# Cross attention of a fused decoder layer: y double-buffered, its scaling and its affine part issued one step earlier

## The reference, cut to what matters

```python
delta = ctx @ Wo.T + bo
delta = rs * delta                       # rs: a clipped scalar
mu, var = delta.mean(-1), ((delta - mu) ** 2).mean(-1)
delta = (delta - mu) / sqrt(var + EPS_LN) * ln_gamma + ln_beta
x2 = layernorm(x1 + delta)               # x1: the input of this block
```

## Time and profile before

| what | value |
|---|---|
| median of 3 executions | 1508.37 us (1506.76 to 1509.74) |
| the profiled execution, its own time | 1507.78 us |
| its span, first to last instruction | 1505.6 us |
| mean granted TensorE clock | 0.974 of full |
| busy: PE, DVE, ACT, POOL | 1398.6, 1206.9, 802.0, 675.5 us |

### The profile page before, as it was taken

One profiled execution on the slowest core, in us unless ns is written; L12 is line 12 of the kernel. 1 busy time (PEld: TensorE's weight loads), 2 busy tenths in 40 slices (PEclk: granted clock), 3 DMA queues, 4 the chain that ended last, 5 costly groups with the idle time before them and its releaser, 6 DMA issues.

```text
span 1505.6 us, 25440 instructions
## 1 busy us (share of the span) xinstructions
PE 1398.6 (93%) x8598; PEld 1098.3 (73%) x8610; DVE 1206.9 (80%) x1979; ACT 802.0 (53%) x1798; POOL 675.5 (45%) x760
## 2 busy tenths in 40 slices
PE   8999999999999999999999999879999998359986
PEld 6888888888888888888888888767777776223332
DVE  6888888888888888888878888636788888669996
ACT  6444444544444445455555565445555665258884
POOL 6534334334335244334333433342445443448984
PEclk9999999999999999999999999989999999679998
DMA  7301101201101011011121111230000004014433
GB/s 267 113 15 43 57 15 30 68 1 42 40 31 42 28 43 29 22 50 56 36 82 66 35 42 35 79 112 15 15 15 15 14 1 175 0 35 91 95 79 93
DMA packets 73477, 79.95 MB, mean 53 GB/s; under 512 B 46102, under 2 KB 46614, under 8 KB 72988
## 3 DMA queue, kind: packets, MB, share of 16 engines
q1 hardware_dynamic: 73372, 78.73, 17.3%
HBM read 59.83 MB, written 8.40 MB: 45 GB/s over the span
## 4 chain that ended last, share of the span: by engine, by line
PE 53%; DVE 29%; issue 9%; POOL 5%; ACT 2%; DMA 1%; DVEq 1%; POOLq 0%; SPq 0%; ACTq 0%
PE psum L342 10%; PE psum L344 9%; PE psum L343 9%; DVE rope_b L541 6%; PE psum L990 4%; PE psum L991 4%; PE psum L992 4%; DVE total_e L554 3%; PE psum L386 3%; DVE acc L584 3%; DVE p L550 3%; DVE s L522 2%; PE psum L1058 2%; PE psum L407 2%; DVE rope_a L541 2%
## 5 line engine op out<-in xcount | busy, mean ns | idle before, releaser
L774 POOL TENSOR_TENSOR qk<-rope_a,rope_b 128x512 f32<-128x512 f32 x128 | 176.7, 1381 | 549.0 <-DVE rope_b L541 549.0
L342 PE MATMUL psum<-x_hi,w_hi 128*128 128x512 f32 x512 | 209.9, 410 | 1.4 <-DVE x_lo L482 1.4
L344 PE MATMUL psum<-x_hi,w_lo 128*128 128x512 f32 x512 | 201.0, 393 | 0.0
L343 PE MATMUL psum<-x_lo,w_hi 128*128 128x512 f32 x512 | 200.0, 391 | 0.0
L541 DVE SCALAR_TENSOR_TENSOR rope_b<-psum,qk_bias,sin 64x512 f32<-64x512 f32 x256 | 191.9, 750 | 3.8
L640 ACT ACTIVATE e<-s 128x384 f32<-128x384 f32 x128 | 66.3, 518 | 229.7 <-DVE s L522 229.7
L522 DVE SCALAR_TENSOR_TENSOR s<-psum,tri 128x384 f32<-128x384 f32 x128 | 70.7, 553 | 120.3 <-PE psum L386 120.2
L342 PE MATMUL psum<-w_hi,x_hi 128*128 128x256 f32 x512 | 147.5, 288 | 1.2 <-DVE v L564 1.2
L343 PE MATMUL psum<-w_lo,x_hi 128*128 128x256 f32 x512 | 144.7, 283 | 0.0
L344 PE MATMUL psum<-w_hi,x_lo 128*128 128x256 f32 x512 | 144.6, 282 | 0.0
L654 ACT ACTIVATE e<-p 128x128 f32<-128x128 f32 x128 | 39.3, 307 | 184.6 <-DVE p L550 184.6
(11 more groups left out here) (187 smaller groups left out, 3796.8 us busy)
## 6 DMA issues: line engine op xcount, KB each, us to landing
stage<-w_self_dram SPq DMA_DIRECT2D x64, 256.0 KB, 2.9
w_raw<-w_ffn_dram SPq DMA_DIRECT2D x32, 512.0 KB, 3.6
acc<-x_dram SPq DMA_DIRECT2D x4, 1024.0 KB, 6.0
w_signs<-w_sign SPq DMA_DIRECT2D x16, 256.0 KB, 2.1
c_raw<-ctxT_dram SPq DMA_DIRECT2D x8, 512.0 KB, 3.5
xstage<-w_cross_dram SPq DMA_DIRECT2D x16, 256.0 KB, 3.0
w<-w_signs SPq DMA_DIRECT2D x2, 2048.0 KB, 11.9
out_dram<-yb SPq DMA_DIRECT2D x16, 256.0 KB, 2.1
```

The costliest lines, as they stand in the source:

```text
L342: pe.matmul(ps, ah, bh, start=n == 0, stop=False)
L343: pe.matmul(ps, ah, bl, start=False, stop=False)
L344: last = pe.matmul(ps, al, bh, start=False, stop=n == len(pairs) - 1)
L774: nc.gpsimd.tensor_tensor(qk[:, k % 2, which, :], rope_a[:, which, :], rope_b[:, which, :], ALU.add).then_inc(qk_ready, 1)
```

## The change

y gets a second buffer. `take_y(b)` then waits only for `finish_y` of element b-2. ScalarE's `scale_y(b-1)` is issued at the start of step 3 of body b, ahead of the exponentials of chunk 3, where it was issued at the start of body b+1. GpSimd's `finish_y(b-1)` is issued at the end of step 3 of body b, behind the split of chunk 2, where it was issued in step 0 of body b+1, behind the split of chunk 3. No instruction is added or taken away.

```diff
-        y = sb("y", [P, 2, D])
+        y = sb("y", [P, 2, 2, D])
             def take_y(b, par, j):
                 dve.wait_ge(o_mm, b * 2 + j + 1)
-                wait(dve, summed, b * 2)
+                wait(dve, summed, b * 2 - 2)
                 ps = psP[1] if isinstance(b, int) and (b, j) == (B - 1, 1) else psO
-                nc.vector.tensor_tensor(y[:, j, :], ps[:, :], ob[:], ALU.add).then_inc(y_out, 1)
+                nc.vector.tensor_tensor(y[:, par, j, :], ps[:, :], ob[:], ALU.add).then_inc(y_out, 1)
...
-                statistics(1, b, j, y[:, j, :], (z_done, b * 2))
+                statistics(1, b, j, y[:, par, j, :], (z_done, b * 2))
...
-                tile, res = y[:, 1, :], acc[:, TILES - 1, :]
+                tile, res = y[:, (B - 1) % 2, 1, :], acc[:, TILES - 1, :]
...
-            def scale_y(b):
+            def scale_y(b, par):
...
-                    nc.scalar.activation(y[:, j, :], y[:, j, :], ACT.Identity, scale=rstd_s[:, j:j + 1],
+                    nc.scalar.activation(y[:, par, j, :], y[:, par, j, :], ACT.Identity, scale=rstd_s[:, j:j + 1],
...
-                    if i == 0 and live(b, 2):
-                        scale_y(b - 2)
+                    if i == 3 and live(b, 1):
+                        scale_y(b - 1, 1 - par)
                     if live(b):
                         exps(b, par, i, 0)
...
-                    tile = y[:, j, :]
+                    tile = y[:, par, j, :]
...
                         split_o(pb, par if i else 1 - par, pc)
-                    if i == 0 and live(b, 2):
-                        finish_y(b - 2, par)
+                    if i == 3 and live(b, 1):
+                        finish_y(b - 1, 1 - par)
```

## The result

The changed kernel takes 1512.08 us in the median of 20 executions (1509.04 to 1515.43), the kernel before 1508.79 us (20 executions). The ratio is 1.0022, 95% interval 1.0015 to 1.0030: 3.3 us slower, 2.3 to 4.5. A second timing gave 1.0025 (1.0015 to 1.0034).

The account below looks back on a forecast made before the run. TensorE, busy 93% of the span and never idle in bodies 1 to 6, was taken as the bound. Stall +3.75 and tail -0.5 gave +3.25 us, a forecast median of 1511.6 us, with 8 in 10 between 1507.8 and 1514.6.

Parts of the forecast that it names:

- The stall in bodies 1 to 5: Step 3: scale_y delays take_q, so TensorE waits before project_q(b, 3); 0.75 us a body, +3.75 us in sum.
- what is spared at the start of a body: ScalarE's 2.45 us before the first exponentials lies beside a busy TensorE, so it gains 0.
- GpSimd in the bodies: Full bodies: finish_y delays the split of chunk 3, hidden with 0.5 to 1.3 us left; cost 0, bound +0.3 a body.
- Body 7: finish_y delays the splits: TensorE waits 1.8 us before output(6, 0), and output(7, 0) starts 1.0 us later.
- T: Time of take_y(6, 1) in body 7, taken as 1277.6, 2.0 us earlier than before; bounds 1277.05 and 1278.3.
- rival B: End of the stage: TensorE keeps the 2.4 GHz level through body 7 into 8, total about -1 us; chance 0.10.
- Body 8: take_y(7, 1) no longer trails TensorE's outputs, which take 8.04 us; it comes 0.5 us earlier than before.
- rival E: The clock stays low in body 8 or the stage behind: +2 to +4 us more, 1514.6; chance 0.12.
- A: The forecast itself, whole kernel: +2.0 to +5.0 us slower; chance 0.55.
- The shared resource: VectorE's x2_norm and GpSimd's finish_y share ports, 3.05 us together against 1.00 alone; expected to just miss each other.
- Rival D: Bodies 2 to 5: GpSimd reaches finish_y before x2_norm, VectorE loses 2.05 us each; up to +4, 1515.6; chance 0.08.
- C: The stall in the bodies doesn't show, they stay at 36.4 us; only the tail's gain is left, 1507.6; chance 0.12.

Follow-up runs that it names:

- e2: The changed kernel with the second tile's scaling moved behind the last exponentials of step 3; 1.0001 of the kernel before.
- e1: The changed kernel with GpSimd's affine part back in its old place, ScalarE still scaling early; 1.0003 of the kernel before.
- e3: The kernel before plus only the second buffer of y, scaling and affine part in their old places; 0.9973 of the kernel before.
- e7: Second buffer only, plus unread matmuls: 21 and 15 in bodies 7 and 8, 78 behind the last output, 8 behind the transposes; 0.9931 of the kernel before.
- e0: The changed kernel timed and profiled once more, nothing altered; 1.0025 of the kernel before.
- e5: The changed kernel plus 70 unread matmuls behind the last output projection; 1.0024 of the kernel before.
- e4: Second buffer of y only, plus 70 unread matmuls behind the last output projection; 0.9979 of the kernel before.
- e8: Second buffer of y only, timed again on another chip; 0.9974 of the kernel before.

## Why the prediction was right, and where its sizes were off

- **The stall in bodies 1 to 5**: forecast 5 x 0.75 = 3.75, measured 3.40. Cause and place were right: `take_q(4, 1)` was forecast to end 35.43 us into body 4 and ended at 35.36; e2 takes the stall away by shortening what is ahead of `take_q`, e1 shows that GpSimd has no part in it. Each changed body is 0.74 us longer than body 6, which has no stall: 0.64 of wait and 0.10 of slower matmul, as forecast. The 0.35 too much lies in the step "what is spared at the start of a body", put at 0. Bodies 3 to 5 of before were 0.05 to 0.13 us longer than the others, also in e3, which keeps `scale_y` there (36.36 to 36.47); in e2 (36.32 to 36.35) and in the changed kernel (37.05), where it is gone from there, they are hardly longer or no longer than bodies 1 and 2. So that place had cost 0.3 us in sum.
- **Nothing gives it back**: "nothing gives it back, as TensorE is never idle there" held.
- **GpSimd in the bodies**: margin forecast 0.5 to 1.3 us, measured 1.0, no cost. e1 agrees.
- **Body 7**: the wait is turned into one of TensorE for o_lo, forecast 1.8 us, measured 1.57. take_y(6, 1) was taken at T = 1277.6, 18.98 us into the body, from the middle of full and low clock; it came at 18.35, the full-clock end of the bound. The low spell under output(6, 1) is gone, as is the 2.16 us gap ahead of it. That part of rival B happened; its main part, the high level in body 8, did not.
- **Body 8**: the last split behind the affine part, forecast "some 6 us" of wait, measured 6.49; e1 prices GpSimd's new place at 4.05 us of the end. output(7, 0) was 0.3 and not 1.0 us late, the outputs took 7.8 and not 8.04 us, so take_y(7, 1) came 1.54 us earlier and not 0.5. This is a term of the sum that was mis-sized, by 1.0 us: some 0.6 from T, some 0.2 from the shorter outputs. To the last `x2_norm` the end gained 1.74 us and not 0.5.
- **Behind the stage**: the sum had nothing there. The low level at the start of the feed-forward block lasts longer and takes 2.2 us; it is rival E, "the stage behind", forecast at 0.12 with +2 to +4. It came together with A. Summed, 3.40 - 1.74 + 2.22 = 3.9, against 3.25 forecast and 3.3 measured. That the total was hit so closely is in part luck: the gain at the end was forecast 1.2 us too small, the loss behind it was missing from the sum, and these two errors have opposite signs.
- **The shared resource**: `x2_norm` and `finish_y` missed each other in body 7, and at the end of body 8 they overlapped for 1.95 us in place of 3.05, while one step of `finish_last` (plus beta) took 1.57 us in place of 0.69. No time hangs on it: from take_y(7, 1) to the last `x2_norm` it is 13.44 us, before 13.64. Rival D didn't happen: in the full bodies of the changed kernel the two instructions of `x2_norm` take 0.54 us each, as before. C fell with the 37.05 us of the bodies.
- **Two small slips in the working**, on which nothing hangs: 1287.29 + 0.42 is T + 8.09 and not T + 8.11; and the lower end of the range is given as 1507.8, while C is worked out as 1507.6 and B as "about -1", which is 1507.4.

What stays open: why the low level under the start of the feed-forward block ends later in the changed kernel. The runs show that it goes with the order of the end (15.2 to 15.4 us three times with the old one, 17.5 to 17.6 four times with the changed, 16.2 to 16.5 four times with the affine part behind the last split and the earlier `take_y`), and that it is the clock (13.44 us in e7, where the level stays high). They don't show what sets the moment.

## What to carry to other kernels

Work moved on an engine with much idle time can still cost, if an instruction that the bound engine waits for stands behind it. Look for the slack of that one instruction (here `take_q` had 0.2 us, on an engine that was 55% busy), add up over the bodies what goes beyond it, and try to put only as much ahead as the slack holds. A wait that a buffer removes comes back if the same edit moves long work ahead of what the chain needs next; the buffer alone gave 4 us, the buffer with its two moves lost 3. And where a stage ends with gaps on TensorE, compare the clock behind the gaps as well, since a few us earlier or later there change what comes behind.

## What the runs showed that I had not expected

The granted clock's low level was worth more than the whole change. With unread matmuls in TensorE's gaps from body 7 to the feed-forward block, the kernel is 10 us faster than before (0.9931); without them it has 0.9974, so 6.5 us of that go with the clock. Filling most of the one long gap (70 matmuls, 3.05 and 1.7 us left open) gave nothing; with it all but filled (1.52 us left open), and the gaps ahead of it too, the level stayed high.

The moment at which the granted clock rises in the feed-forward block repeats. Counted from the start of body 7 it came at 71.5 to 71.9 us in three profiles of before, at 75.1 to 75.2 in the four with the changed end (the changed kernel, e0, e2, e5), and at 68.1 to 68.4 in the four with the earlier last `take_y` (e1, e3, e4, e8). It doesn't follow the stage's end: in the changed kernel the last `x2_norm` came 1.7 us earlier than before and the rise 3.2 us later, in e1 5.8 us earlier and the rise 3.7 us earlier. Nor did the 70 fillers move it: in e4 and e5 the level fell only at 61.4 and 64.8 us, where it fell at 44.2 and 47.8 without them, and it rose at 68.2 and 75.1 as without them.
